# A decoder layer: x loaded transposed as well, q, k and v weights centred once

## What is computed

```python
x = x + _L0_attn_ref(_layernorm(x, axis=-1), ...)
# with
m = jnp.mean(x, axis=axis, keepdims=True)
v = jnp.var(x, axis=axis, keepdims=True)
return (x - m) / jnp.sqrt(v + eps)
# and in attention
q = (x @ wq.T).reshape(b, t, NH2, HALF)
k = (x @ wk.T).reshape(b, t, NH2, HALF)
v = (x @ wv.T).reshape(b, t, H, 2 * HALF)
q = _apply_rope(q, cos, sin)
k = _apply_rope(k, cos, sin)
```

## Time and profile before

| what | value |
|---|---|
| median of 3 runs | 1100.36 us |
| the runs | 1105.04, 1100.36, 1099.93 us |
| the profiled execution, from its first to its last instruction | 1105.1 us |
| instructions | 24352 |
| mean clock granted to PE, as a share of full speed | 0.982 |
| read from DRAM, written | 116.04 MB, 122.00 MB |

### The profile page before, as it was taken

The page is one execution under the profiler, slowest core; times in us unless marked ns, Lnnn a source line. Parts: engine busy times, 40 slices in busy tenths (PEclk is TensorE's granted clock), DMA queues, the critical chain, the costliest instruction groups (busy, mean ns, idle before and its releaser), DMA issues.

```text
span 1105.1 us, 24352 instructions
## 1 busy us (share of the span) xinstructions
PE 1029.0 (93%) x6564; PEld 834.0 (75%) x6564; DVE 830.3 (75%) x2254; ACT 619.2 (56%) x1751; POOL 577.9 (52%) x565
## 2 busy tenths in 40 slices
PE   5998999999999999999999987999999999999992
PEld 4786777878878778777787865888787878778781
DVE  5776687878888788788887865588777777777871
ACT  4554445555555455555545542576666766667661
POOL 3214566666666556666666656434443434434343
PEclk9999899999999999999999998999999999999996
DMA  7999574543313112121121210599999999999974
GB/s 292 368 298 280 176 266 169 203 153 135 123 54 96 48 48 95 48 94 48 51 92 49 77 40 20 174 252 256 247 245 249 254 235 258 238 248 256 253 182 54
DMA packets 94052, 185.75 MB, mean 168 GB/s; under 512 B 24663, under 2 KB 24791, under 8 KB 93504
## 3 DMA queue, kind: packets, MB, share of 16 engines
q1 hardware_dynamic: 62640, 145.13, 41.2%
q0 software_dynamic: 31376, 40.20, 17.7%
HBM read 116.04 MB, written 122.00 MB: 215 GB/s over the span
## 4 chain that ended last, share of the span: by engine, by line
DMA 28%; issue 25%; POOL 22%; DVE 11%; PE 10%; ACT 1%; DVEq 1%; SPq 1%; POOLq 1%; ACTq 0%
DMA layer_out<-qk_both,slot_table 25%; POOL slot_records L544 12%; DVE qk_both L1003 4%; POOL rstd L555 4%; PE ps L1181 4%; POOL layer_out L629 3%; POOL qk_rot L600 2%; PE ps L1166 2%; DVE diff L998 2%; POOL rstd_h L608 2%; DMA x_ln<-in_x 2%; PE ps L1188 1%; DVE st L905 1%; DMA gu_sb<-in_weights 1%; PE ps L1171 1%
## 5 line engine op out<-in xcount | busy, mean ns | idle before, releaser
L544 POOL DMA_INDIRECT slot_records<-row,slot_idx x256 | 259.3, 1013 | 87.9 <-issue 59.9
L629 POOL DMA_INDIRECT layer_out<-qk_both,slot_table x96 | 162.6, 1694 | 232.8 <-DMA layer_out<-qk_both,slot_table 205.5
L555 POOL TENSOR_TENSOR rstd<-mv,neg_half 128x1 f32<-128x1 f32 x96 | 67.8, 706 | 126.7 <-DVE mv L921 78.6
L1181 PE MATMUL ps<-w_high,xn_high 128*128 128x512 f32 x384 | 115.1, 422 | 0.7 <-ACT xn_high L650 0.7
L1337 PE MATMUL ps<-w_high 128*128 128x192 f32 x576 | 90.8, 279 | 19.7 <-DVE w_low L1088 18.4
L1181 PE MATMUL ps<-w_low,xn_high 128*128 128x512 f32 x384 | 108.2, 404 | 0.0
L1181 PE MATMUL ps<-w_high,xn_low 128*128 128x512 f32 x384 | 108.1, 404 | 0.0
L685 ACT ACTIVATE probs<-ps,neg_max 128x128 f32<-128x128 f32 x256 | 89.9, 377 | 32.2 <-DVE neg_max L913 32.2
L1337 PEld LDWEIGHTS ps<-w_high 128*128 128x128 f32 x576 | 76.1, 191 | 39.5 <-issue 38.7
L650 ACT ACTIVATE xn_t<-ps 128x512 f32<-128x512 f32 x64 | 38.3, 599 | 111.4 <-PE ps L1166 111.3
L1088 DVE TENSOR_TENSOR w_low<-gu_sb,w_high 128x1536 fp32r<-128x1536 f32 x48 | 84.4, 1758 | 11.7 <-ACT w_high L650 11.4
(11 more groups left out here) (161 smaller groups left out, 2428.6 us busy)
## 6 DMA issues: line engine op xcount, KB each, us to landing
gu_sb<-in_gate_up SPq DMA_DIRECT2D x48, 768.0 KB, 6.3
slot_records<-dn_both SPq DMA_DIRECT2D x6, 3366.0 KB, 23.6
w_raw<-slot_records SPq DMA_DIRECT2D x48, 280.5 KB, 4.3
dn_both<-in_down_proj SPq DMA_DIRECT2D x48, 256.0 KB, 4.2
x_ln<-in_x SPq DMA_DIRECT2D x32, 256.0 KB, 2.7
x_res<-in_x SPq DMA_DIRECT2D x32, 256.0 KB, 3.0
ctx_t_sb<-in_ctx_t SPq DMA_DIRECT2D x32, 256.0 KB
ctx_sb<-in_ctx_rows SPq DMA_DIRECT2D x32, 256.0 KB
```

What stands on the lines that cost most here:

```text
L544: pool.indirect_dma_start(out=records, out_offset=bass.IndirectOffsetOnAxis(ap=slot_idx[:, s.parity, k:k + 1], axis=0), in_=row[:, s.parit ...
L555: pool.tensor_tensor(rstd[:, :], mv[:, 1:2], neg_half[:, 0:1], ALU.pow).then_inc(steps.sem, 1)
L629: pool.indirect_dma_start(out=out, out_offset=bass.IndirectOffsetOnAxis(ap=slot_table[0:PART[h], 2 * d.index + h:2 * d.index + h + 1], axi ...
L1181: last = pe.matmul(dst, left[:, c, :], right[:, m, c, :], start=(n == 0 and c == 0), stop=(n == 2 and c == KC - 1))
```

## The change

x is also laid out transposed in DRAM, and SP loads both forms of each batch. PE's transposes of xn1, ACT's normalising activation and DVE's shift go away. ACT's xn1_high and DVE's xn1_low are made from the loaded x_t_sb. At the start PE adds up the columns of the q, k and v weights (products with a matrix of ones, four for each weight), and DVE subtracts a 512th of that from the weights before they are split. The deviation comes in twice: ACT scales the rotation table with rstd1 for each batch (rope_now), and scales v's copy. rstd1 has two columns now, one for each parity of the batch. The load of x_t of a batch waits until xn1_low of the batch two before it is made, since that is when its buffer is free. Cut to its core (the list of arguments is left out):

```diff
@@ -137,9 +137,9 @@
         mv1 = sb("mv1", [P, 2])
-        rstd1 = sb("rstd1", [P, 1])
-        shift1 = sb("shift1", [P, 1])
-        xn1 = sb("xn1", [P, 2, DM])
+        rstd1 = sb("rstd1", [P, 2])
+        rope_now = sb("rope_now", [P, 2, 2, NF])
+        x_t_sb = sb("x_t_sb", [P, 2, KC, P])
         xn1_high = sb("xn1_high", [P, KC, P], FP32R)
@@ -260,6 +260,8 @@
         s_rope = sem("rope_table_loaded")
+        s_sums = sem("weight_column_sums_made")
+        s_centred = sem("weights_centred")
         s_split_a = sem("weights_high_made")
@@ -274,16 +276,16 @@
         d_xln = [sem("x_for_norm_loaded0"), sem("x_for_norm_loaded1")]
+        d_xt = [sem("x_transposed_loaded0"), sem("x_transposed_loaded1")]
         d_xres = [sem("x_residual_loaded0"), sem("x_residual_loaded1")]
...
         d_last = [sem(f"last_batch_scattered{n}") for n in range(8)]
-        ln1 = Steps(sem("norm1_vector"), "stats aggr eps shift")
+        ln1 = Steps(sem("norm1_vector"), "stats aggr eps")
         ln1_p = Steps(sem("norm1_pool"), "rstd")
-        ln1_a = Steps(sem("norm1_scalar"), "normed")
-        prj_t = Steps(sem("project_tensor"), "xT q qk v qT kT")
-        prj_a = Steps(sem("project_scalar"), "xT v qT kT")
+        prj_t = Steps(sem("project_tensor"), "q qk v qT kT")
+        prj_a = Steps(sem("project_scalar"), "xT tab v qT kT")
         prj_v = Steps(sem("project_vector"), "low")
@@ -332,6 +334,11 @@
 
+        CENTRED = 3
+
+        def column_sums(m):
+            return ps[:, (4, 5, 7)[m], :]
+
         block = stack.enter_context(nc.Block())
@@ -385,8 +392,10 @@
                     if m == 0:
+                        load_x_t(Batch(0, 0, NB))
                         sp.dma_start(rope_tab[:, :, :, :], cos_sin).then_inc(s_rope, 16)
                 load_x(Batch(0, 1, NB))
+                load_x_t(Batch(0, 1, NB))
 
@@ -450,9 +459,15 @@
                 if n.back(2).exists():
-                    sp.wait_ge(ln1_a.sem, ln1_a.after(n.back(2), "normed"))
+                    sp.wait_ge(ln1.sem, ln1.after(n.back(2), "stats"))
                 sp.dma_start(x_ln[:, n.parity, :], x[bass.ds(n.index * P, P), :])\
                   .then_inc(d_xln[n.parity], 16)
+
+            def load_x_t(n):
+                if n.back(2).exists():
+                    sp.wait_ge(prj_v.sem, prj_v.after(n.back(2), "low"))
+                sp.dma_start(x_t_sb[:, n.parity, :, :], x_t[bass.ds(n.index * P, P), :, :])\
+                  .then_inc(d_xt[n.parity], 16)
 
@@ -462,6 +477,7 @@
                     load_x(n)
+                    load_x_t(n)
                 if c.exists():
@@ -577,7 +593,12 @@
                     scatter(0)
-                scale(ln1_p, ln1, n, rstd1, mv1)
+                if n.exists():
+                    pool.wait_ge(ln1.sem, ln1.after(n, "eps"))
+                    if n.back(2).exists():
+                        pool.wait_ge(prj_a.sem, prj_a.after(n.back(2), "v"))
+                    pool.tensor_tensor(rstd1[:, n.parity:n.parity + 1], mv1[:, 1:2], neg_half[:, 0:1], ALU.pow)\
+                        .then_inc(ln1_p.sem, 1)
                 if early:
@@ -652,17 +673,26 @@
             def split(m):
-                act.wait_ge(d_w[m], 16)
+                if m < CENTRED:
+                    act.wait_ge(s_centred, m + 1)
+                else:
+                    act.wait_ge(d_w[m], 16)
                 act.activation(w_high[:, m, :, :], raw(m), ACT.Copy).then_inc(s_split_a, 1)
...
             def turn(b):
-                n, p, a, c, r = (b[k] for k in ("norm", "project", "attend", "cross", "route"))
+                p, a, c, r = (b[k] for k in ("project", "attend", "cross", "route"))
                 if p.exists():
-                    act.wait_ge(prj_t.sem, prj_t.after(p, "xT"))
+                    act.wait_ge(d_xt[p.parity], moved(p, 1))
                     if p.back(1).exists():
...
                         act.wait_ge(prj_v.sem, prj_v.after(p.back(1), "low"))
-                    copy(xn1_high[:, :, :], blocks(bank_ta), prj_a)
+                    copy(xn1_high[:, :, :], x_t_sb[:, p.parity, :, :], prj_a)
+                    act.wait_ge(ln1_p.sem, ln1_p.after(p, "rstd"))
+                    if p.first():
+                        act.wait_ge(s_rope, 16)
+                    if p.back(1).exists():
+                        act.wait_ge(rope.sem, rope.after(p.back(1), "sin"))
+                    copy(rope_now[:, :, :, :], rope_tab[:, :, :, :], prj_a, scale=rstd1[:, p.parity:p.parity + 1])
                 if p.first():
@@ -689,13 +719,6 @@
                     copy(xn3_t[:, :, :], blocks(bank_tb), rte_a)
-                if n.exists():
-
-                    act.wait_ge(ln1.sem, ln1.after(n, "shift"))
-                    if n.back(2).exists():
-                        act.wait_ge(prj_t.sem, prj_t.after(n.back(2), "xT"))
-                    act.activation(xn1[:, n.parity, :], x_ln[:, n.parity, :], ACT.Identity, bias=shift1[:, :],
-                                   scale=rstd1[:, :]).then_inc(ln1_a.sem, 1)
                 if c.exists():
@@ -723,7 +746,7 @@
                         act.wait_ge(att_t.sem, att_t.after(p.back(2), "pv"))
-                    copy(v_sb[:, p.parity, :], bank_v, prj_a)
+                    copy(v_sb[:, p.parity, :], bank_v, prj_a, scale=rstd1[:, p.parity:p.parity + 1])
                 if p.exists():
@@ -790,6 +813,12 @@
         def _(dve):
+            def centre(m):
+
+                dve.wait_ge(s_sums, m + 1)
+                dve.scalar_tensor_tensor(raw(m), column_sums(m).unsqueeze(1).to_broadcast([P, KC, DM]), -1.0 / DM,
+                                         raw(m), ALU.mult, ALU.add).then_inc(s_centred, 1)
+
             def split(m):
@@ -895,7 +924,7 @@
                         dve.wait_ge(prj_t.sem, prj_t.after(p.back(1), "v"))
-                    dve.tensor_tensor(xn1_low[:, :, :], blocks(bank_ta), xn1_high[:, :, :].bitcast(FP32),
+                    dve.tensor_tensor(xn1_low[:, :, :], x_t_sb[:, p.parity, :, :], xn1_high[:, :, :].bitcast(FP32),
                                       ALU.subtract).then_inc(prj_v.sem, 1)
@@ -941,7 +970,7 @@
                     if n.back(1).exists():
-                        dve.wait_ge(ln1_a.sem, ln1_a.after(n.back(1), "normed"))
+                        dve.wait_ge(ln1_p.sem, ln1_p.after(n.back(1), "rstd"))
                     dve.bn_stats(st1[:, :], x_ln[:, n.parity, :]).then_inc(ln1.sem, 1)
@@ -967,11 +996,6 @@
                                              ALU.mult, ALU.mult).then_inc(att_v.sem, 1)
-                if n.exists():
-
-                    dve.wait_ge(ln1_p.sem, ln1_p.after(n, "rstd"))
-                    dve.scalar_tensor_tensor(shift1[:, :], mv1[:, 0:1], -1.0, rstd1[:, :],
-                                             ALU.mult, ALU.mult).then_inc(ln1.sem, 1)
                 if c.exists():
@@ -1002,15 +1026,14 @@
                         buf[:, :, :, :].rearrange("p (a g) r f -> p a (g r) f", a=2), qk,
-                        rope_tab[:, i, :, :].unsqueeze(2).to_broadcast([P, 2, 2 * NH2, NF]), ALU.mult)\
+                        rope_now[:, i, :, :].unsqueeze(2).to_broadcast([P, 2, 2 * NH2, NF]), ALU.mult)\
                         .then_inc(rope.sem, 1)
-                if p.first():
-                    dve.wait_ge(s_rope, 16)
                 if p.exists():
...
                         dve.wait_ge(rope_p.sem, rope_p.after(p.back(1), "imag_k"))
+                    dve.wait_ge(prj_a.sem, prj_a.after(p, "tab"))
                     rotary(qk_cos, 0)
@@ -1082,7 +1105,13 @@
                     setup_router()
-            turns(dve, turn, lambda: split(0))
+            
+            def first_weights():
+                for m in range(CENTRED):
+                    centre(m)
+                    if m == 0:
+                        split(0)
+            turns(dve, turn, first_weights)
 
@@ -1189,11 +1218,6 @@
                 p, a, c, r = b["project"], b["attend"], b["cross"], b["route"]
-                if p.exists():
-                    pe.wait_ge(ln1_a.sem, ln1_a.after(p, "normed"))
-                    if p.back(1).exists():
-                        pe.wait_ge(prj_a.sem, prj_a.after(p.back(1), "kT"))
-                    transpose4(bank_ta, lambda k: xn1[:, p.parity, k * P:(k + 1) * P]).then_inc(prj_t.sem, 1)
                 if r.first():
@@ -1251,8 +1275,6 @@
                     pe.wait_ge(crs_v.sem, crs_v.after(c, "normed"))
-                    if p.exists():
-                        pe.wait_ge(prj_v.sem, prj_v.after(p, "low"))
                     transpose4(bank_ta, lambda k: xn2[:, k * P:(k + 1) * P]).then_inc(crs_t.sem, 1)
@@ -1315,6 +1337,12 @@
                     gate_columns()
+            pe.wait_ge(s_made, 1)
+            for m in range(CENTRED):
+                pe.wait_ge(d_w[m], 16)
+                for c in range(KC):
+                    last = pe.matmul(column_sums(m), ones[:, :], raw(m)[:, c, :], start=(c == 0), stop=(c == KC - 1))
+                last.then_inc(s_sums, 1)
```

(3 more changed lines are left out.)

## The result

The changed kernel takes 1116.57 us in the median (1111.75 to 1121.45, 6 runs) beside 1102.80 for the kernel before (1099.93 to 1106.17, 6 runs on the same chip): a ratio of 1.0135, 95% interval 1.0111 to 1.0160. It is slower, by 13.8 us; 11 had been forecast, as 1111 on a median of 1100.36.

What follows compares the result with a forecast made beforehand. Steady turns were taken as bound by a ring of DVE and POOL, early turns by DMA transfers. Steady turns 0, start 9 (fills) to 11 (compute), loss of step 1: +11 on 1100.36 gives 1111 us, range 1101 to 1120.

Steps and rivals of the forecast that it cites:

- Compute of the start: Sums and centrings on DVE's path: first rotary products 11.8 us later, at 31.3; compute 11 us late, ends 8 and 12.
- The first sums: Column sums of the first weight on PE at the start: 6.5 us, from 3.4 at full pace to 6.9 at half.
- SP's hold: In the start x_t's load waits for xn_low: first fill at 29.1 us, 15 late; fills' end moves about 9.
- the hole in the transfers: Gap in the start's DMA transfers while SP is held: 24.8 - 20 = 5 us.
- The loss of step between fills and compute: Added in the start because fills and compute come late by nearly the same: 1 us.
- Steady turns: In the loop PE loses 0.59 us per turn, 18.9 in all; 0 taken as gain, ends 0 and -18.9.
- PE's waits for heads_low and xprobs_t grown by about 0.6 us per turn together: Steady-turn sign that the forecast is right: PE spends the removed transposes' time waiting at these two places.
- No piece of PE is in that ring: In the steady pair the chain of waits runs over DVE and POOL only; a turn takes 19.7 us.
- a little slack: In steady turns PE is put in step by DVE; it waits for xprobs_t 0.25 us each in 22 turns.
- B: Rival: PE bounds steady turns, 0.59 us gained in all 32; -8 us, 1092; turn below 19.35 us; chance 0.08.
- C: Rival: in the start DVE's 10.5 us of waiting covers compute's 11; about +1 or 2, 1102; chance 0.12.
- D: Rival: xn_low on DVE collides with POOL in each turn, +0.38 us, 12 us in all, 1123; chance 0.08.

Runs made afterwards that it cites:

- e1: Changed kernel without the column sums and the centring, so x's mean stays in: 1106.73 us, ratio 1.0038 to the kernel before.
- e2: Changed kernel with the load of x_t last in SP's turn, behind late loads and record fills: 1110.84 us, ratio 1.0061 to the kernel before.
- e7: Changed kernel with e5's edit, x_t's load last, first fill ahead of the late loads and second in the same turn: 1105.16 us, ratio 1.0002.
- e3: Changed kernel with four unread transposes put back on PE at the head of each turn: 1121.82 us, ratio 1.0170 to the kernel before.
- e5: Changed kernel with xn_low on POOL and DVE's weight into the row, its address and key moved behind neg_max: 1110.26 us, ratio 1.0050.
- e6: Changed kernel with x_t's load last, first fill ahead of the late loads and second in the same turn: 1113.90 us, ratio 1.0075.
- e9: Changed kernel with e5's edit, x_t's load last, second weight centred earlier, first fill behind small late loads, last fill a turn earlier: 1113.71 us, ratio 1.0060.
- e12: Changed kernel with e5's edit, x_t's load last, and the second weight centred ahead of the first low part: 1104.07 us, ratio 0.9986.
- e8: Kernel before with the first fill ahead of the late loads and the second in the same turn: 1106.93 us, ratio 1.0022.
- e10: Kernel before with the first fill ahead of the last weight's wait and the last fill one turn earlier: 1119.80 us, ratio 1.0106.
- e11: Kernel before with an unused buffer of rope_now's size ahead of xn1: 1107.18 us, ratio 1.0001.
- e4: Changed kernel with xn_low moved from DVE to POOL, at the head of POOL's turn: 1138.30 us, ratio 1.0332 to the kernel before.

## Why the prediction was right

**Direction and cause: right, and shown.** The loss lies in the start; e1 takes most of it away (13.8 us to 3.1), with nothing else altered.

**Compute of the start.** Predicted first rotary products 31.3, 11.8 late; measured 29.29 in that profile, and 30.4 to 32.0 in e2 to e7, which have the same sums and centrings. The first sums took 5.4 us (6.47 to 11.83) for 6.5: the sums of one weight are eight instructions, and the first of them follow each other at 0.75 to 0.99 us, the rest at 0.43. In the other runs with sums they took 5.2 to 6.6, as the pace changes at 9.3 us in one and at 12.2 in another: 6.5 lay at the upper end, not outside. The other steps came as written: 2.29 and 2.28 for a centring, 1.91, 2.29, 0.68.

For what comes then the prediction took 4.17 us from the trace of before, where the clock is full. But PE stands 2.81 us for xn_low, up to 23.44, and from 23.5 to 26.9 us its granted clock is 0.51, the lower level; from the low part of weight three to the rotary products 3.78 us pass. In e2, e3, e5, e6 and e7 PE stands 2.5 to 3.5 us in one piece, the lower clock lasts 6.8 us, and 5.2 to 5.7 us pass. In e9 and e12, where the second weight is centred first, PE's stand is broken in two of at most 1.6 us, the clock stays full, and it is 3.33. That is more than half of the spread of the first rotary products, and what the order of centring gained.

That no centring hides behind the weights' arrival is seen in DVE's list.

**SP's hold: right in place, too small in size.** First fill predicted at 29.1, measured at 28.06. I let 9 of the 15 us arrive, on the ground that the hole in the transfers was 24.8 - 20 = 5 us. That step failed: what SP had issued before its stand had landed by 16 us, not 20, and little moved before 30, so the hole was some 14 us, where the kernel before has one of 4 (a share of 0.10 and 0.09 from 14 to 18). What arrived can be read at x_ln of batch 5: issued at 83.39, against 70.01 in the kernel before, 13.4 later. So nearly the whole delay was kept, inside the stated end of 19. The loss of step between fills and compute, put at 1, was 4.2 (batch 4, 13.97 less 9.76): DVE stood up to 6.1 us at x_ln. That the sum came near is in part luck: it took 10 (between 9 and 11) and 1, and 10 and 4 less 2 came, so that the fills' larger delay and what was given back partly cancel.

**Steady turns: 0 taken, 0.06 gained per turn.** From batch 8 to the last the lateness falls from 14.29 to 12.49, 1.8 of 18.9 us. Up to batch 28 it falls by 0.12 to 0.13 per pair, and nearly all of that lies at one place in DVE's list, xn2 behind rstd2: two turns in a row of the kernel before, then of the changed one.

```profile
457.38 0.55 DVE L991 TENSOR_SCALAR xn<-x,mv,rstd 128x512 f32<-128x512 f32 x1 [0.72 <-POOL rstd L555]
...
477.25 0.55 DVE L991 TENSOR_SCALAR xn<-x,mv,rstd 128x512 f32<-128x512 f32 x1 [0.84 <-POOL rstd L555]
```

```profile
470.83 0.55 DVE L1015 TENSOR_SCALAR xn<-x,mv,rstd 128x512 f32<-128x512 f32 x1 [0.71 <-POOL rstd L571]
...
490.59 0.55 DVE L1015 TENSOR_SCALAR xn<-x,mv,rstd 128x512 f32<-128x512 f32 x1 [0.71 <-POOL rstd L571]
```

In every second turn of the loop xn2 starts 0.24 us after rstd2 has ended in the kernel before, e8, e10 and e11, else 0.13; it is 0.13 in all turns of the loop with x_t, e3's among them, where PE has its transposes. So this gain is not PE's. The shift, which stood a few instructions before xn2, is gone; whether that is the cause no run shows. The last 0.6 us, in the last three turns, can be PE's: e3, with the transposes back, loses 1.15 there.

PE did absorb its time, but not as the step said: 0.23 of the 0.59 went into the wait for k_t, which the step did not name, and the sign "PE's waits for heads_low and xprobs_t grown by about 0.6 us per turn together" came at 0.28: 8.7 + 4.1 us in 22 turns, for 1.2 + 5.5 before. "No piece of PE is in that ring" holds for the chain shown; that PE has "a little slack" was too strong. e3 shows that, with the transposes, PE's ring is the longer one by 0.39 per pair at the products' new pace; at the old pace (96 products, 0.003 us each) that is 39.35, an estimate, beside the 39.36 of the kernel before. The two rings were about level: the zero was right because DVE's ring is as long, not because PE had slack.

**Rivals.** B needed a turn below 19.35: not the case (19.6); even e5, with DVE relieved, stays at 19.4. C fell to the place of the fills, as the prediction said it must (the wait for scattered records ends at 126.6 us, not at 112), and e2 shows that it would hold otherwise. D did not come: the median of xn_low is 0.685 us for 0.684 (one of 32 took 1.43), and e4 shows, on a neighbouring instruction, what POOL's reading of SBUF beside DVE can cost.

## What to carry to other kernels

Work moved out of a loop into the start pays only if the loop was bound by it: here 18.9 us of PE time went with 1.8 us less of attention, most of that not PE's, and the start's price was paid in full. When a queue gets a new wait, ask what stands behind it: one load's place in SP's list was worth 0.7% here (1.0135 to 1.0061), for no work at all. Where transfers fill the DMA engines, an earlier place for one is a later place for another, so name the second wait before moving the first.

## What the runs showed of the hardware that was not expected

The products of the projections start 0.231 us apart in the median in the kernel before (724 distances, 200 to 600 us) and 0.234 in the changed one (723), also those of the output projection, whose data did not change; e1 to e7, e9 and e12 are at 0.234, e8, e10 and e11 at 0.231. Over 48 products that is 0.14 us a turn, a quarter of what the transposes gave back. e1 rules out the centred weights and e11 the shift of the buffers by rope_now; the cause stays open.

A 48-column instruction on DVE can take 1.97 us for 0.24 (e4), and the cost shows in a line that the edit did not touch. And an issue on SP can take as long as a transfer when large transfers stand before it: layer_out behind a fill took 9.24 us in the changed kernel, two fills 22.84 in e9.
